# A two-layer mixture-of-experts kernel: where in a tick the means of the first eight ticks' weight matrices are taken, and four smaller moves of order at the start

## The reference

```python
# first layer: expert by token id, the four experts' matrices are ctx[e]
h = layernorm(x)
e = minimum(clip(token_ids, 0, 24999) // 6250, 3)
x1 = x + (silu(h @ ctx[e].T) * (h @ ctx[e].T)) @ ctx[e].T
# second layer: expert = argmax of router logits, ternary weights, int8-like activations
g = bitlinear(h2, wg[e]); u = bitlinear(h2, wu[e])      # h2 = layernorm(x1), 8 experts
out = x1 + bitlinear(square(relu(g)) * u, wd[e])
# bitlinear(x, w): w -> clip(round(w / m), -1, 1) * m with m = mean(|w|); x -> round(x * s) / s, s = 127 / max|x|
```

## Time and profile before

| | |
|---|---|
| median of 3 runs | 272.07 us (271.14 to 274.15) |
| the profiled execution | 271.92 us, its span 270.1 us |
| mean granted TensorE clock | 0.975 |
| start of PE's tick 2, 3, 4, 5 | 36.01, 45.84, 54.61, 67.85 us |
| DMA | 51.72 MB, mean 191 GB/s |

### The profile page before, as it was taken

How to read it: one execution, slowest core, us unless ns; L and a number is a source line. 1 busy time by engine, 2 the same in 40 slices (tenths; PEclk the granted TensorE clock), 3 DMA queues, 4 the chain that set the end, 5 groups by cost and what they waited for, 6 DMA issues and landing times.

```text
span 270.1 us, 5804 instructions
## 1 busy us (share of the span) xinstructions
PE 239.6 (89%) x1410; PEld 176.1 (65%) x1420; DVE 215.5 (80%) x680; ACT 210.7 (78%) x322; POOL 164.7 (61%) x318
## 2 busy tenths in 40 slices
PE   2296888959999999999999999989979999999980
PEld 2144667748888888888888888877535555555530
DVE  5967879748789988778978887777769899999971
ACT  1866759549888789988888988894788999999960
POOL 4463545537676767686776776365746568556553
PEclk9999799988999999999999999997999999999997
DMA  6969921755544566584655643443168688411110
GB/s 211 413 237 354 426 115 39 305 236 187 163 178 173 197 227 201 219 299 189 208 224 195 223 164 144 178 158 99 54 200 292 197 276 289 155 70 67 61 38 0
DMA packets 13839, 51.72 MB, mean 191 GB/s; under 512 B 2862, under 2 KB 2862, under 8 KB 10224
## 3 DMA queue, kind: packets, MB, share of 16 engines
q1 hardware_dynamic: 8928, 37.91, 38.5%
q0 software_dynamic: 4880, 13.44, 14.4%
HBM read 40.49 MB, written 13.48 MB: 200 GB/s over the span
## 4 chain that ended last, share of the span: by engine, by line
PE 72%; DVE 9%; DMA 7%; issue 5%; POOL 2%; ACT 2%; SPq 0%; POOLq 0%; DVEq 0%; ACTq 0%
PE bank L1354 36%; PE bank L1463 17%; PE bank L1343 8%; PE bank L1435 5%; DMA x<-x_rows,gather 4%; PE bank L1457 3%; DVE ctx_lo L860 2%; POOL out_rows L555 1%; DMA x_rows<-row,store_at 1%; DMA late_rows<-x_rows 1%; DVE hT_lo L947 1%; DVE p L954 1%; DVE stats L918 1%; PE bank L1373 1%; DMA token_ids<-token_ids_in 1%
## 5 line engine op out<-in xcount | busy, mean ns | idle before, releaser
L1463 PE MATMUL bank<-ternary,qT 128*128 x179 | 43.4, 380 | 0.5 <-issue 0.2
L595 ACT ACTIVATE ternary<-staged 128x2048 bf16<-128x2048 f32 x20 | 38.3, 1916 | 3.5 <-DMA staged<-weight_chunks 3.4
L508 POOL DMA_INDIRECT x_rows<-row,store_at x19 | 24.6, 1294 | 15.5 <-POOL store_at L500 9.5
L601 ACT ACTIVATE ternary<-staged,w_scale 128x1536 int16<-128x1536 f32 x20 | 31.3, 1565 | 0.0
L1463 PEld LDWEIGHTS bank<-ternary,qT 128*128 128x128 bf16 x184 | 17.7, 97 | 20.8 <-issue 4.8
L555 POOL DMA_INDIRECT out_rows<-late_rows x18 | 19.5, 1086 | 16.2 <-DVE late_rows L1180 13.7
L452 POOL DMA_INDIRECT x<-x_rows,gather x19 | 21.2, 1117 | 12.2 <-DVE row L974 5.8
L1354 PE MATMUL bank<-ctx_hi,hT_hi 128*128 x76 | 24.2, 443 | 2.6 <-DVE hT_lo L947 1.4
L954 DVE SCALAR_TENSOR_TENSOR p<-bank,rstd,p 128x512 f32<-128x512 f32 x19 | 14.3, 750 | 14.4 <-ACT p L648 14.4
L1463 PE MATMUL bank<-ternary,rT 128*128 x87 | 22.6, 380 | 1.0 <-ACT rT L695 0.8
L1354 PE MATMUL bank<-ctx_hi,pT_hi 128*128 x76 | 23.3, 429 | 0.0
(11 more groups left out here) (217 smaller groups left out, 665.6 us busy)
## 6 DMA issues: line engine op xcount, KB each, us to landing
staged<-weight_chunks SPq DMA_DIRECT2D x20, 1024.0 KB, 5.6
late_rows<-x_rows SPq DMA_DIRECT2D x18, 260.0 KB, 3.2
ternary<-ctx_chunks SPq DMA_DIRECT2D x4, 1024.0 KB, 10.1
ternary<-weight_chunks SPq DMA_DIRECT2D x4, 1024.0 KB, 6.7
x_rows<-filler SPq DMA_DIRECT2D x9, 260.0 KB, 2.9
staged<-x_rows SPq DMA_DIRECT2D x5, 260.0 KB, 2.9
x<-x_rows,gather POOLq DMA_INDIRECT x19, 3.6
x_rows<-row,store_at POOLq DMA_INDIRECT x19, 3.3
```

The costliest lines, as they stand in the source:

```text
L508: pool.indirect_dma_start(x1_rows, bass.IndirectOffsetOnAxis(ap=store_at[b % ROWS][:, :], axis=0), row[b % ROWS][:, :], None, bounds_check ...
L595: nc.scalar.activation(ternary[:, m * K * D:(m + 1) * K * D], staged_of(i), ACT.Abs, accum_out=abs_sum[:, 2 * i:2 * i + 1]).then_inc(abs_r ...
L601: nc.scalar.activation(ternary[:, m * K * D + DVE_COLS:(m + 1) * K * D].bitcast(I16), staged_of(i)[:, DVE_COLS:], ACT.Copy, scale=w_scale[ ...
L1463: last = pe.matmul(ps[:, :], left[:, k * P:(k + 1) * P], ternary[:, bass.ds(e * (3 * K * D) + (kind * K + k) * D, D)], start=(k == 0), sto ...
```

## The change

- PE: in ticks 2 to 7 (`t < SETTLED`) `sum_mean(t + 2)` is the tick's last instruction. From tick 8 on it stands where it stood. `sum_mean(2)` comes behind the transposes of h(2), `sum_mean(3)` behind the first product of tick 2.
- DVE: in these ticks mean, scale and `scale_part` of matrix t+2 stand at the tick's end; cuts shift by one matrix until tick 8. Ahead of the ticks `low_half(1, 0)` stands before the statistics of block 1, `scale_part(1)` before `pT_rest(0)`, mean and scale of matrix 2 behind the statistics of block 2, and those of matrix 3 move into tick 2.
- ACT: in these ticks `scale_part(t + 2)` stands behind `evict_hT(t + 1)`; ahead of them `silu(0)`, `evict_hT(1)` and `evict_pT(0)` stand before `sum_abs(2)`, and `silu(1)`, `evict_hT(2)` before `scale_part(2)`; `sum_abs(4)` and `scale_part(3)` move into tick 2.
- PE: the first product of block 1 also begins with its high halves, and waits for the low halves between the groups.
- SP: context 2 is loaded before matrix 2; the filler rows are written after matrix 5 and not 4; the first split matrix is loaded after matrix 6 and not 5.

```diff
+SETTLED = 8
@@ sync
             sp.wait_ge(gathering, 2)
+            load_context(2)
             load_weights(2)
-            load_context(2)
             load_weights(3)
             load_context(3)
             for i in range(4, len(ORDER)):
                 load_weights(i)
-                if i == 4:
+                if i == 5:
                     sp.wait_ge(made, 12)
                     sp.dma_start(x1_rows[FILLER_BLOCK:SCRATCH_ROWS], filler[:, :]).then_inc(filler_out, 16)
-                if i == FIRST_PIECE[0] + ABOVE:
+                if i == FIRST_PIECE[0] + ABOVE + 1:
                     sp.wait_ge(ctx_lo_ready, E1)
                     sp.dma_start(extra, weights_in[EXTRA[0]]).then_inc(extra_in, 16)
@@ scalar
             scale_part(1)
-            sum_abs(2)
             silu(0)
             evict_hT(1)
             evict_pT(0)
+            sum_abs(2)
+            silu(1)
+            evict_hT(2)
             scale_part(2)
             sum_abs(3)
-            silu(1)
-            evict_hT(2)
-            scale_part(3)
-            sum_abs(4)
             for t in range(2, TICKS):
                 evict_pT(t - 1)
+                if t == 2:
+                    sum_abs(2 + ABOVE)
                 square(t - 2)
-                if t > 2:
+                if t >= SETTLED:
                     scale_part(t + ABOVE)
                 silu(t)
                 evict_x1T(t - 2)
                 evict_hT(t + 1)
                 if t == 2:
-
+                    scale_part(3)
+                if t < SETTLED:
                     scale_part(t + ABOVE)
                 if t in EXTRA_SCALES:
                     scale_piece(*EXTRA_SCALES[t])
@@ vector
             low_half(0, 1)
             hT_rest(0)
+            low_half(1, 0)
             moments_of(1)
             aggregate(1)
             normalise(1)
             variance(1)
-            low_half(1, 0)
             scale_part(0)
             gate(0)
             hT_rest(1)
             low_half(1, 1)
-            mean_of(2)
-            scale_of(2)
+            scale_part(1)
             pT_rest(0)
-            scale_part(1)
             moments_of(2)
             aggregate(2)
             normalise(2)
             variance(2)
+            mean_of(2)
+            scale_of(2)
             low_half(2, 0)
             gate(1)
             hT_rest(2)
             low_half(2, 1)
             scale_part(2)
-            mean_of(3)
-            scale_of(3)
             moments_of(3)
             aggregate(3)
             variance(3)
-            scale_part(3)
@@ vector, the ticks
-                if t > 2:
+                if t >= SETTLED:
                     mean_of(t + ABOVE)
...
-                if t > 2:
+                if t >= SETTLED:
                     scale_of(t + ABOVE)
...
                 normalise(t + 1)
+                if t == 2:
+                    mean_of(3)
+                    scale_of(3)
...
                 if t == 2:
-                    mean_of(t + ABOVE)
-                    scale_of(t + ABOVE)
-                scale_part(t + ABOVE)
+                    scale_part(3)
+                elif t >= SETTLED:
+                    scale_part(t + ABOVE)
...
                 aggregate(t + 2)
                 variance(t + 2)
+                if t < SETTLED:
+                    mean_of(t + ABOVE)
+                    scale_of(t + ABOVE)
+                    scale_part(t + ABOVE)
...
-                if 5 <= t < 9:
+                if 5 <= t < 8:
                     cut(t - 5)
+                if t == 9:
+                    cut(3)
...
-                cut(t + ABOVE)
+                if 2 < t <= SETTLED:
+                    cut(t + ABOVE - 1)
+                if t >= SETTLED:
+                    cut(t + ABOVE)
@@ tensor
-            def product1(ps, hi, lo, e, first=False):
+            def product1(ps, hi, lo, e, b=None):
                 pairs = [(hi, ctx_hi), (hi, ctx_lo), (lo, ctx_hi)]
                 for n, (left, right) in enumerate(pairs):
-                    if first and n == 1:
+                    if n == 1 and b == 0:
                         pe.wait_ge(ctx_lo_ready, 1)
-                    if first and n == 2:
-                        pe.wait_ge(hT_lo_ready, 1)
+                    if n == 1 and b == 1:
+                        pe.wait_ge(ctx_lo_ready, e + 1)
+                    if n == 2 and b in (0, 1):
+                        pe.wait_ge(hT_lo_ready, b + 1)
@@ tensor, the order
             transpose_h(1)
-            sum_mean(2)
             transpose_p(0)
             first_product(1)
             load_expert(2)
             transpose_h(2)
-            sum_mean(3)
+            sum_mean(2)
             second_product(0)
             for t in range(2, TICKS):
                 transpose_p(t - 1)
-                if t > 2:
+                if t >= SETTLED:
                     sum_mean(t + ABOVE)
                 first_product(t)
                 load_expert(t + 1)
                 if t == 2:
-                    sum_mean(t + ABOVE)
+                    sum_mean(3)
                 rank(t - 3)
...
                 logits(t - 2)
                 count_in(t - 3)
+                if t < SETTLED:
+                    sum_mean(t + ABOVE)
```

More of the change, by code:

```diff
@@ L1386, in first_product @@
                     return
-                if b == 0:
-                    pe.wait_ge(hT_hi_ready, 1)
-                    pe.wait_ge(ctx_hi_ready, 1)
+                if b < 2:
+                    pe.wait_ge(hT_hi_ready, b + 1)
+                    pe.wait_ge(ctx_hi_ready, b + 1)
                     pe.wait_ge(centred, 1)
@@ L1393, in first_product @@
                     pe.wait_ge(hT_lo_ready, b + 1)
-                if b >= 2:
                     pe.wait_ge(p_ready, b - 1)
-                if 1 <= b < E1:
+                if 2 <= b < E1:
                     pe.wait_ge(ctx_lo_ready, expert_of[b] + 1)
@@ L1401, in first_product @@
                     pe.wait_ge(ctx_lo_ready, E1)
-                product1(a_ps[b % 2], hT_hi, hT_lo, expert_of[b], b == 0).then_inc(a_ready, 1)
+                product1(a_ps[b % 2], hT_hi, hT_lo, expert_of[b], b).then_inc(a_ready, 1)
             def transpose_p(b):
```

## The result

The changed kernel takes 284.7 us (median of 4 runs, 283.37 to 285.12) against 272.03 before: a ratio of 1.0446, 95% interval 1.0376 to 1.0515. The forecast was 280.5 with a range of 274 to 287.5, slower by over 1% at 87%.

What follows compares the result with a forecast made beforehand. PE was taken to bound the kernel from tick 5, other limits, including DMA waits, before. The profiled 271.9, plus 6.25 for tick 9 starting later, plus 2.3 for clock falls, gave 280.5 us; range 274 to 287.5.

Steps and rivals of the forecast that it cites:

- third rival: The clock falls in all of ticks 4 to 8, 7.5 us instead of 2.3: 285.7, with late gather 288.4; 22%.
- ACT link: Behind PE's sum, ACT runs scale_part, sum_abs, sometimes sum_piece, then evict_pT in program order, done 5.26 us after the sum starts.
- The unit, 10.5 us a tick: Ticks 5 to 7: from one PE sum_mean to the next takes 10.5 us instead of 8.0, +7.5 in all.
- ACT's ring: Loop from PE's sum through scale, ACT's queue to evict_pT, DVE's h and PE's second product to the next sum: 10.5 us.
- Tick 8, 11.65: Old order returns; PE's sum of matrix 10 waits for ACT's sum_abs(10) behind scale_part(9): 11.65 us, +3.65.
- The start, tick 3 at 41.7: Up to tick 3: earlier silu(0) and block 1's product start tick 3 at 41.7 against 45.84, -4.1 us.
- Tick 4, 11.35: Tick 4 runs from 51.6 to 62.95, with x(5)'s gather issued at 45.7 and taken to land at 51.
- the upper bound of 8: Flight time of x(5)'s gather in tick 4, bounded by 3.6 and 8.0 us; 8 us would add 2.7.
- The clock, 2.3 us: PE's clock falls between one and two times of a possible 0 to 5 in ticks 4 to 8, 1.5 us each.
- the first (the wait only goes away): Ticks 3 to 8 all take PE's 8.0 us, as DMA no longer holds PE: 261.9 us; 4%.
- S+3.9: S is when PE starts sum_mean(t+2); pT_hi before 3.9 us after it would decide for the faster rival; forecast S+5.2.
- The second: Rival that loop and gain cancel: undisturbed part, gather at 49.3, no clock fall give 276.5, another 2 us within 1%; 9%.

Runs made afterwards that it cites:

- e1: Kernel before, with only the means of ticks 3 to 7 moved to the tick's end and scale_part behind evict_hT; 287.2 us, 1.0559.
- e2: Changed kernel with SETTLED = 3: means in their old place from tick 3 on, start, loads and block 1 as changed; 269.7 us, 0.991.
- e3: Changed kernel, but in ticks 3 to 7 ACT sums matrix t+2 (and the piece) in the same tick, ahead of scale_part; 279.3 us, 1.0284.
- e6: Changed kernel with 33 unread matmuls added in PE's idle stretches in ticks 4 to 8; 282.0 us, 1.0372.
- e5: Changed kernel, but in tick 7 ACT sums matrix 10 ahead of scale_part(9); 281.2 us, 1.0325.
- e4: Changed kernel with a buffer of its own for x(5), so its gather is issued at 43.05 instead of 47.20; 283.3 us, 1.0398.
- e7: e2, but in tick 2 ACT sums matrix 5 ahead of scale_part(4); 269.1 us, 0.9895.
- e11: e8 with SP's order of before: matrix 2 ahead of context 2, filler rows behind matrix 4, split matrix ahead of matrix 6; 271.75 us, 0.9972.
- e9: Kernel before with only a buffer of its own for x(5), gathered ahead of the loads; 273.5 us, 1.0077.
- e8: e7 with a buffer of its own for x(5), gathered ahead of the loads; 264.2 us, 0.9727.

## Why the prediction was right

- **The number**: 284.7 against 280.5, or 12.7 us slower where 8.4 were forecast. It lies 4.2 us above the forecast and 1.0 under the third rival's 285.7; the range held it because its upper end allowed for the clock falling each time and for a late gather. The mechanism was right, and two terms of the sum were too small: the landing of x(5)'s gather in tick 4, and the clock.
- **The sign and the mechanism**: shown. e1 has the loss with the move alone, e2 none of it without, e3 takes the ACT link out and tick 5 falls to 8.31.
- **The unit, 10.5 us a tick**: 10.60 in ticks 6 and 7, and in all three of e6. Each step stood within about 0.1 us. What the forecast lacked is the second ring behind the first (residual, gather, statistics, mean on DVE), which e3 brought out; it changes nothing while ACT's ring is longer.
- **Tick 8, 11.65**: 11.75 at full clock in e6. Right; that it is the border's price and not the move's own, e5 shows, where tick 8 takes 9.51.
- **The start, tick 3 at 41.7**: 42.45. Product 1 began at 25.19 (25.1 forecast), its second group at 27.23 (26.3). low_half(1, 1), taken at 1.2 us, took 1.84; scale_part(1) behind it, taken at 1.15, took 0.47. The two errors cancel on DVE, so h(2) and the second product 0 came as forecast (30.12 for 30.05). The time was lost at product 2, which waited for low_half(2, 1) and began at 34.76 for 34.1: of these 0.66 us 0.45 are that instruction, 1.66 long where the earlier trace rows gives 1.215. DVE's and POOL's timelines of the changed kernel:

```profile
25.26 1.84 DVE L863 TENSOR_TENSOR ctx_lo<-ternary,ctx_hi 128x1024 fp32r<-128x1024 f32 x1
27.02 0.47 DVE L882 TENSOR_SCALAR ternary<-staged,w_scale 128x512 int16<-128x512 f32 x1
...
30.57 1.21 DVE L863 TENSOR_TENSOR ctx_lo<-ternary,ctx_hi 128x1024 fp32r<-128x1024 f32 x1
...
32.95 1.66 DVE L863 TENSOR_TENSOR ctx_lo<-ternary,ctx_hi 128x1024 fp32r<-128x1024 f32 x1
```

```profile
24.13 1.88 POOL L461 CAST ctx_hi<-ternary 128x2048 fp32r<-128x2048 f32 x1
31.09 2.45 POOL L461 CAST ctx_hi<-ternary 128x2048 fp32r<-128x2048 f32 x1 [5.07 <-DMA ternary<-ctx_chunks]
```

  Where two of these overlap, it is the one that began later that grew. The low halves of 25.26 and 32.95 began inside a copy and ended 1.1 us behind its end (26.01 and 33.54), about their own length. The low half of 30.57 began ahead of the copy and kept its 1.21; the copy took 2.45 for 1.88. The Trainium skill's rule in GPSIMD Engine Reference, Specifications, that GpSimd contends with Vector instructions with two SBUF inputs as well, agrees with this. The forecast had let the rows of before decide against it; but there low_half(1, 1) began at 26.87, ahead of the copy of 27.35, and it was the copy that grew, to 2.49.
- **Tick 4, 11.35**: 13.54. The failed step is the gather of x(5): taken as issued at 45.7 and landed at 51, it was issued at 47.20 and landed at 54.07. The start's 0.75 us and the 0.8 us between the residual's end and POOL's issue were left out, and the flight, taken at 5.3 us, took 6.9 with two loads beside it; the upper bound of 8 (2.7 us more) was nearly the case. That moves tick 5 from 62.95 to 65.97, just short of the 66 that the forecast had named as a sign of being wrong. e4 gives 1.3 us of it back, the rest being there a fall of the clock.
- **The clock, 2.3 us**: three falls, in ticks 4, 5 and 8, where between one and two were taken. By e6 they cost 0.3, 1.6 and 2.0 us, 3.9 together; the size of one (1.5) was near where it lay on the path. How many there would be was a guess, and no run shows what decides it. Against the forecast's 106.1, tick 9 starts at 113.1. Of these 7.0 us 3.0 come from start and tick 4 (tick 5 at 65.97, not 62.95), 3.6 from the falls in ticks 5 and 8, and 0.4 from ticks of 10.60 and 11.75. Behind tick 9, 0.8 us come back: there the changed kernel has no counterpart to the fall at 181 to 182, with PE at full clock through the same instructions.
- **The signs**: PE's transposes of h waited 2.1 us a tick for DVE's h and tick 8 waited 3.45 us for ACT's sum, as forecast. ACT's wait for w_scale was named as 2 to 3 us; it was 5.18, 3.57 and 3.57.
- **The rivals**: the first (the wait only goes away) fell, and it fell at the place named: pT_hi came at S+5.3, not before S+3.9. The second needed an early gather and a full clock, and had neither. The third was half true: the clock fell in three of its five ticks, and its time was nearer than the forecast's.

## What to carry to other kernels

When an instruction is moved behind the end of a stage, follow what every other engine holds behind its result, in program order, until the chain comes back to the instruction itself; the length of that ring, not the wait that was removed, is the new period. A wait that goes may only have covered the next (e2 and e7), and where two orders meet, the instruction that both sides need pays once more (tick 8, and e5's cure: take the sum ahead of the step that waits). Try removals in pairs before one is called worthless: here the early gather cost 2.1 us on the kernel before, the exchange of the sum gave 0.4 us on e2, and both together gave 5.0 there. The early gather alone on e2 was not run, so how much of the 5.0 needs both is open.

## What the runs showed of the hardware

The granted clock fell from 2.4 to 1.2 GHz (PEclk 1.00 to 0.50) in tick 5 of the changed kernel, in which PE was busy for 9.81 of 12.21 us. Ahead of the fall, from 69.2 to 72.7 us, PE had transposes, one small product and 2.4 us without work. The clock fell between 73 and 74 us and was at 0.50 to 77, with product matmuls running since 72.69; columns here are stretch, length, PE, PEld, DVE, ACT, POOL busy, clock, DMA share, GB/s:

```profile
73.00:74.00 1.00, 1.00 (x5) 0.82 (x4) 0.92 (x4) 0.57 (x1) 0.89 (x2) 0.83 0.10 37
74.00:77.00 3.00, 3.00 (x8) 2.35 (x8) 1.18 (x4) 0.00 (x0) 1.95 (x6) 0.50 0.00 0
```

Ticks 6 and 7, with the same order of instructions and about the same idle time, kept full clock, and in e4 it was tick 6 that lost it. With 33 matmuls that nobody reads, placed in idle time (e6), it stayed at 1.00 in ticks 4 to 8, and the kernel was 2.0 us faster by the ratios and 3.2 by the profiled spans.

A DVE instruction with two SBUF inputs that took 1.2 us alone took 1.84 and 1.66 us when it began inside a POOL copy, 2.83 in e11 and 2.89 in e9, where it began 0.1 us behind the copy's start. Each time it ended 1.1 us behind the copy. Where it began first it kept 1.2 us, and the copy, 1.88 us alone, took up to 2.6 (e8).
